# Second graph attention: leaky relu split into a per-node linear word and a fused relu-product

## The reference, cut to what matters

```
x_l = x @ W_l
x_r = x @ W_r
e = leaky_relu(x_l[src] + x_r[dst], 0.2) @ att          # src, dst with one self loop per node added
e_exp = exp(e - segment_max(e, dst)[dst])
alpha = e_exp / segment_sum(e_exp, dst)[dst]
out = segment_sum(alpha[:, None] * x_l[src], dst) + bias
```

## Time and profile before

| what | us |
|---|---|
| time, median of 3 runs | 4915.72 |
| lowest and highest run | 4913.82, 4917.73 |
| the profiled execution's own time | 4920.97 |
| span of that execution in the profile | 4919.2 |
| node work ahead of the second attention (`own_scores` and parts) | 3118.4 to about 3136 |
| second attention, from its first gather to its last copy | 3148.9 to about 4558 |

### The profile page before, as it was taken

How to read it: one execution, slowest core, us unless ns; L and a number is a source line. 1 busy time by engine, 2 the same in 40 slices (tenths; PEclk the granted TensorE clock), 3 DMA queues, 4 the chain that set the end, 5 groups by cost and what they waited for, 6 DMA issues and landing times. The chain is left out here.

```text
span 4919.2 us, 75233 instructions
## 1 busy us (share of the span) xinstructions
PE 2366.5 (48%) x18851; PEld 1748.8 (36%) x18904; DVE 2934.1 (60%) x5736; ACT 547.8 (11%) x1369; POOL 2696.2 (55%) x2730
## 2 busy tenths in 40 slices
PE   0133333333316623666666665355545555554698
PEld 0033333333215512444444444233333333333232
DVE  8631111111138856888888886688888888888201
ACT  0000000000014400111111111011111111111000
POOL 0037777777735405777777772376665666663000
PEclk9955555555555555565556565555555555555899
DMA  0122222222125414444444441232332333231744
GB/s 21 37 89 76 76 76 73 76 76 77 51 45 106 92 31 106 117 118 116 115 119 113 116 117 38 50 78 69 71 72 65 70 74 71 69 71 47 261 168 172
DMA packets 473580, 428.19 MB, mean 87 GB/s; under 512 B 207198, under 2 KB 364148, under 8 KB 473194
## 3 DMA queue, kind: packets, MB, share of 16 engines
q1 hardware_dynamic: 214266, 235.47, 16.0%
q0 software_dynamic: 81072, 115.39, 11.1%
q10 hardware_dynamic: 178048, 75.47, 5.6%
HBM read 322.46 MB, written 105.27 MB: 87 GB/s over the span
## 5 line engine op out<-in xcount | busy, mean ns | idle before, releaser
L1341 POOL DMA_INDIRECT rows<-nodes_xl,id_slot x832 | 861.3, 1035 | 643.4 <-issue 244.4
L1341 POOL DMA_INDIRECT rows<-nodes_kv,id_slot x832 | 848.9, 1020 | 347.5 <-issue 244.4
L607 POOL DMA_INDIRECT msg_by_src<-message,place_slot x832 | 826.7, 994 | 346.1 <-issue 252.8
L1674 PE MATMUL counts_p<-hot_blocks 128*128 128x128 bf16 x2080 | 539.9, 412 | 347.4 <-DVE running_counts L1539 347.4
L581 PE MATMUL picked<-X,hotT 128*128 x1664 | 374.3, 423 | 668.4 <-DVE hotT L564 668.4
L557 DVE TENSOR_TENSOR message<-picked,w_dst 128x512 f32<-128x512 f32 x104 | 71.9, 692 | 907.5 <-ACT message L594 897.1
L581 PEld LDWEIGHTS picked<-X,hotT 128*128 128x128 f32 x1664 | 360.5, 331 | 682.1 <-issue 682.1
L1715 PE MATMUL sums<-parts,hot 128*128 128x68 bf16 (+1 forms) x4992 | 325.3, 251 | 390.3 <-DVE parts L1528 390.3
L1715 PEld LDWEIGHTS sums<-parts,hot 128*128 128x128 bf16 x4992 | 311.8, 168 | 439.5 <-issue 439.5
L1674 PEld LDWEIGHTS counts_p<-hot_blocks 128*128 128x128 bf16 x2080 | 277.7, 148 | 525.2 <-DVE running_counts L1539 376.7
L1539 DVE SCALAR_TENSOR_TENSOR running_counts<-running_counts,same_block,counts_p 128x128 f32<-128x128 f32 x1040 | 359.9, 346 | 161.7 <-PE counts_p L1674 25.9
(11 more groups left out here) (344 smaller groups left out, 3716.2 us busy)
## 6 DMA issues: line engine op xcount, KB each, us to landing
adjacency<-running_counts ACTq DMA_DIRECT2D x1040, 64.0 KB
loc_all<-loc_by_cell SPq DMA_DIRECT2D x104, 512.0 KB
loc_all<-loc_by_cell SPq DMA_DIRECT2D x208, 256.0 KB
blocks<-adjacency SPq DMA_DIRECT2D x40, 1280.0 KB
rows<-msg_by_src SPq DMA_DIRECT2D x312, 68.0 KB
blocks<-adjacency SPq DMA_DIRECT2D x20, 960.0 KB
msg_by_src<-message,place_slot POOLq DMA_INDIRECT x832
ef_slot<-efT_in SPq DMA_DIRECT2D x416, 32.0 KB
```

The source lines that it names most:

```text
L607: pool.indirect_dma_start(out=msg_dram, out_offset=bass.IndirectOffsetOnAxis(ap=ids[:, s, t:t + 1], axis=0), in_=rows[:, s, t, :], in_offs ...
L1341: pool.indirect_dma_start(out=rows[:, j, t, :], out_offset=None, in_=table, in_offset=bass.IndirectOffsetOnAxis(ap=ids[:, j, t:t + 1], axis=0)
L1674: ins = nc.tensor.matmul(counts_p[:, q - HALVES[half][0], :], hot_b[:, r, 1, :, t], hot_b[:, r, 0, :, t], start=g == 0, stop=g == 1)
```

## The change

The leaky relu is written as 0.2 y + 0.8 relu(y). With y = x_l[src] + x_r[dst], the part 0.2 y @ att falls into a term of the source, 0.2 x_l @ att, and one of the destination, which is the same for all edges of a destination and is left out of the softmax. `own_scores` computes the source's term for all nodes and puts it into a 66th word of each row of `nodes_xl`; it also makes `att_r` = 0.8 att once. In `gat` one instruction does max with 0 and the product with `att_r`, in place. The sum over 64 follows, and a last instruction of 128x8 adds the word from the gathered row. The buffer `leaky` goes. The number of instructions in `gat` stays four, and the waits that count them (`gat, 4`) stay.

```diff
-        nodes_dram = {k: dram(f"nodes_{k}", [NPAD, w]) for k, w in (("kv", 2 * D + HEADS), ("xl", D + 1))}
+        nodes_dram = {k: dram(f"nodes_{k}", [NPAD, w]) for k, w in (("kv", 2 * D + HEADS), ("xl", D + 2))}
...
-            xl = sbuf("xl", [P, NT, D + 1], ctx=c)
+            xl = sbuf("xl", [P, NT, D + 2], ctx=c)
+            att_r = sbuf("att_relu", [P, D], ctx=c)
...
-                    step(v.memset(xl[:, :, D:], 1.0))
+                    step(v.memset(xl[:, :, D:D + 1], 1.0))
+                    step(v.tensor_scalar(att_r[:], att_s[:], 0.8, None, ALU.mult))
+                    step(v.tensor_tensor(sq[:], lr[:, :, 0:D], rowwise(att_s[:]), ALU.mult))
+                    step(v.tensor_reduce(a[:], sq[:], AX.X, ALU.add))
+                    step(v.tensor_scalar(xl[:, :, D + 1], a[:], 0.2, None, ALU.mult))
                     step(v.tensor_copy(xl[:, :, 0:D], lr[:, :, 0:D]))
                     step(v.tensor_tensor(sq[:], lr[:, :, 0:D], lr[:, :, D:2 * D], ALU.add))
-                    step(v.scalar_tensor_tensor(sq[:], sq[:], 0.2, sq[:], ALU.mult, ALU.max))
-                    step(v.tensor_tensor(sq[:], sq[:], rowwise(att_s[:]), ALU.mult))
+                    step(v.scalar_tensor_tensor(sq[:], sq[:], 0.0, rowwise(att_r[:]), ALU.max, ALU.mult))
                     step(v.tensor_reduce(own_s[:], sq[:], AX.X, ALU.add))
+                    step(v.tensor_tensor(own_s[:], own_s[:], xl[:, :, D + 1], ALU.add))
...
-            leaky = sbuf("score_b", [P, TB, D], ctx=c2)
...
                 step(v.tensor_tensor(product[:], picked, rows[:, :, 0:D], ALU.add))
-                step(v.scalar_tensor_tensor(leaky[:], product[:], 0.2, product[:], ALU.mult, ALU.max))
-                step(v.tensor_tensor(product[:], leaky[:], att_s[:].unsqueeze(1).to_broadcast([P, TB, D]), ALU.mult))
+                step(v.scalar_tensor_tensor(product[:], product[:], 0.0, att_r[:].unsqueeze(1).to_broadcast([P, TB, D]),
+                                            ALU.max, ALU.mult))
                 step(v.tensor_reduce(to, product[:], AX.X, ALU.add))
-            attend(1, nodes_dram["xl"], D + 1, 0, D + 2, near, gat, 4, False, None, (BFIRST * STEPS, BSECOND), acc)
+                step(v.tensor_tensor(to, to, rows[:, :, D + 1], ALU.add))
+            attend(1, nodes_dram["xl"], D + 2, 0, D + 2, near, gat, 4, False, None, (BFIRST * STEPS, BSECOND), acc)
```

## The result

The changed kernel takes 4887.1 us, median of 4 runs (4885.65 to 4887.84), against 4916.73 for the kernel before (4 runs, 4913.82 to 4919.74). The ratio is 0.9938 with an interval of 0.9924 to 0.9952. The gain is 29.6 us, where 50 were forecast, and 4887.1 lies above the range of 4857 to 4875. The direction was right and the size was not.

The account below looks back on a forecast made before the run. It took DVE's queue to bound the second attention from step 4 on. -52.1 us in the loop and +2.5 in `own_scores` made -49.6, so 4866.1 us from 4915.72; range 4857 to 4875.

Parts of the forecast that it names:

- the cost of the loop's instructions: Scoring in each step: relu of 0.692 us removed, 128x8 instruction of 0.171 added, 0.521 saved; 52.1 us over 100 steps.
- The line of the Trainium skill on S2S2D2_STT: Rival 1: the fused scoring instruction runs at half rate, 1.225 us, so no change, about 4920 us; chance 0.04.
- the node work: Instructions added once in `own_scores`, on DVE alone between barriers: 2.5 us more, all on the path.
- PE and the gather: Second attention: PE's work stays in DVE's shadow; 264-byte rows cost POOL's gather nothing, 42.5 us a window against DVE's 51.3.
- rival 2: The gather becomes the bound if one takes over 1.60 us; at 1.70, about 4942 us; chance 0.04.
- rival 3: At s = 0 DVE waits for PE's turned scores, so one step in four loses its saving: 4879.7 us; chance 0.08.
- Five waits for rows: DVE's waits for gathered rows at the start remain, those of steps 1 to 4 together about 2 us longer.
- the reading of DVE's idle time: Second attention: DVE's other idle time is some 0.03 us behind each chained instruction, and register loads such as 0.25 us.
- the term for added code: Four more instructions in `own_scores` cost their durations and four gaps of 0.03 us, 0.12, within the 2.5 us.
- an instruction taken from that queue shortens it by its full length: From step 4 on the second attention is as long as DVE's queue, so removed instructions save their full length.
- a new wait ahead of L1442 or of the scores: Sign that the prediction is wrong: DVE shows such a wait in the steady part.
- POOL's wait for `mixed`: POOL's wait until DVE frees ring slots should fall from 242.8 us by some 50 to about 190.

Follow-up runs that it names:

- s3: s1 with the changed scoring, but own_scores of as many instructions as before (source's linear term left out): 4839.60 us, -52.9 against s1.
- s4: The changed kernel with eight memsets ahead of the loop and one of three bf16 parts in PE's pick and scatter: 4843.02 us, -49.5 against s1.
- s1: The kernel before with PE's work cut in both attentions, one of three bf16 parts in pick and scatter: 4892.48 us.
- s2: The changed kernel with PE's work cut to one of three bf16 parts in pick and scatter: 4859.17 us, -33.3 against s1.
- e2: The kernel before with four one-column memsets at the end of own_scores' arithmetic, ahead of the loop: 6282.02 us, 1.0042 of before (6256.03).
- e5: The same kernel as e2 on another chip: 6315.94 us, 1.0036 of the kernel before (6292.86).
- e10: The kernel before with four one-column memsets ahead of the loop, on a third chip: 6329.25 us, 1.0031 of before (6303.67).
- f3: The kernel before with four memsets ahead of the loop, in the last round: 6284.14 us, 1.0047 of before (6254.89).
- e4: The changed kernel with a hint on DVE's loop, in both attentions, that it will jump back: 6245.77 us, 0.9983 of before (6256.03).
- e7: The same kernel as e4 on another chip: 6286.75 us, 0.9988 of the kernel before (6292.86).
- f2: The changed kernel with DVE's loop marked in both attentions, in the last round: 6247.98 us, 0.9987 of before (6254.89).
- fourth round: Runs of s1 to s4, all with PE's work cut, on a chip where the kernel before with all of PE's work takes 4922.92 us.

## Why the prediction was right, and where it failed

**Right: the cost of the loop's instructions.** Fused 0.692 for 0.704, 128x8 0.172 for 0.171. An ordinary step is 0.52 us shorter, as worked out, and s3 gives 52.9 us, where the same terms make 53.7. L406 in the earlier trace rows was the right row to go by. The line of the Trainium skill on S2S2D2_STT (page "Vector Engine (DVE) Microarchitecture Reference", section "7. Points that are easy to get wrong") would have had some 1.2 us by the prediction's estimate, and the trace again disagrees, with 692 ns.

**Right: the node work.** In DVE's timeline it goes from 3116.44 to 3127.60, 11.16 us, where before it went from 3118.38 to 3126.99, 8.61. That is 2.55 more, and 2.5 was forecast.

**Right: PE and the gather.** DVE's wait for counts stayed at 20.5 us and POOL's gather fell to 1020 ns from 1035, so neither rival 2 nor rival 3 took place, although 4887.1 is nearer to the time of rival 3 (4879.7) than to the forecast. Five waits for rows remain, 1.7 us longer in all, where 2 was said.

**Failed: the reading of DVE's idle time, and with it the term for added code.** The step that failed is "an instruction taken from that queue shortens it by its full length": the sum put the place of the loop's code at nothing. The prediction took DVE's idle time as gaps of 0.03 us and register loads, and gave the four added instructions of `own_scores` their durations and nothing else. The list of waits had a line that speaks against the first: `hotT` idle for 27.7 us in 11 times, released by "issue", with up to 2.7 us each, which no register load has in the earlier trace rows. Eleven is the count of the loop's jumps. With that line read, the next question would have been how far the code ahead of the loop moves, and the sum would have had a term for it, of either sign. The runs showed that term: 22.9 us of stops ahead of `hot_blocks` in place of 3.7 at the running counts, and 4.2 more ahead of `hot`. The prediction had said that a new wait ahead of L1442 or of the scores would show it wrong; the new one came at another place, ahead of `hot_blocks`.

**The sum again, by rows.** From step 5 to step 103 the scores start 1309.97 us apart before (4526.96 - 3216.99) and 1279.76 in the changed kernel. In DVE's timeline of the latter these are

```profile
3215.01 0.68 DVE L2015 TENSOR_TENSOR score_a<-picked,rows 128x512 f32<-128x512 f32 x1
```

```profile
4494.77 0.69 DVE L2015 TENSOR_TENSOR score_a<-picked,rows 128x512 f32<-128x512 f32 x1
```

So 98 steps gained 30.2 us where 98 x 0.521 = 51.1 were due, and 20.9 are missing. Rows for them: +22.9 for the stops ahead of `hot_blocks`, -3.7 + 0.2 for those at the running counts that went, -1.4 at `hotT`, and +4.2 ahead of `hot` (10.4 for 6.2). That is 22.2. That the 4.2 hang on the code's place too, and not on the short instruction ahead, is shown by s3 and s4, which have that instruction and 6.2 us. The rest, -1.3, is in the lengths of instructions that the change does not touch: three small groups (L1461, L1462, L1494) take 10 to 23 ns more each in the changed kernel, some 1.3 us in all, and do so in s3 and s4 too; two others (L1443, L1458) take 1.0 us less, and `hotT` takes 503 ns instead of 518, 1.6 us less in all. Why these lengths move is not known.

POOL's wait for `mixed` fell by 17.1 us to 225.7, not by 50 to 190. DVE didn't shorten by 50. But the size would not have come out then either: with PE's work cut the wait goes from 241.3 (s1) to 197.2 (s2), 164.4 (s3) and 156.3 (s4), so it falls by 77 us in s3, where the time falls by 53. What else goes into it is not settled.

**What stays open.** The changed kernel with the eight memsets, or with the loop marked, was not timed on a chip like the first with all of PE's work in it. So that the missing 20 us of the real pair come from the place of the code is carried over from s1 to s4 and from the stops in its own trace. The first should give some 16 us more than the change by s4, which is an estimate. The marked loop clears both stops in the trace, 27 + 20 us of idle time on DVE, but on the chips that it ran on its time was that of the eight memsets within 4 us, so what it gives is not known. Why the stops cost time there (e2, e5, e10, f3: 23 to 29 us) while the saving in the scores is nearly lost is argued, not shown: a saving in a step ends in the wait for PE's counts, and the stop at the loop's start seems to lie outside that cover. Why these chips differ is not known either, nor what the mark on the loop changes, so that no code is fetched.

## What to carry to other kernels

Count the waits that end in "issue": when their number is the number of a loop's jumps, look in the DMA view whether a packet of instructions comes at the same moments. If so, they are probably fetches of code. Any instruction added or removed on that engine ahead of the loop can then move the second stop under long work or out from under it. So time an edit of a loop alone and with a few idle instructions ahead of it, before the difference is put down to the edit. Whether the order of work at the loop's start can be chosen to cover the stop was not tried.

## What the runs showed of the hardware

- A jump back of this loop, which fetches five or six packets of 8.2 KB in a pass, stops DVE for 2.4 to 2.8 us (27.7 us in 11 jumps), and a second stop of up to 2.3 us follows if a block's border comes before there is work to cover it. Four memsets ahead of the loop made the whole second stop, 11 times, 20 us (e2, f3: 19.9; e5: 20.7; e10: 20.8).
- A border further on in the pass seems to cost some 0.35 us: the gaps ahead of `hot` are 10.4 or 6.2 us in all over 24 times, with the same instructions around them, and twelve of them grew.
- A loop marked for its jump has neither stop: 27 us ahead of `hotT` become 0.2 (e4, e7, f2), and no packet of its code comes in ten passes (f2).
- The kernel before takes 4917 and 4923 us in the first comparison and in the fourth round, and 6255 to 6304 on four other chips. On these PE stands for over 200 us in 1900 with nothing to wait for ahead of its picks (3.6 us in the changed kernel on the first), at about the same granted clock (0.56 against 0.59).
